# One store moved to the end of each step of the load queue, in an adaptive feed-forward kernel of two layers

## The reference, cut to what matters

```
x = x + L0_ffn( L0_cond(x, cond_128, ...), L0_ffn_weight )
    # L0_cond: grouped convolution along the columns, 9 taps, 4 groups, plus a context term and a bias
    # L0_ffn:  both sides rounded to int8 with a scale per row, product over 1024 columns, scaled back to f16
x = x + L1_ffn( L1_cond(x, cond_128, ...), W, b, A, Bmat, LiMEs )
    # L1_cond: a small MLP gives each batch mixing weights of 8 banks; a 64x64 matrix mixes the channels ("tokens") of each batch
    # L1_ffn:  H = tokens @ W.T + b, and z = tokens @ A; a gate over 8 experts scales z; result H + (z * mix) @ Bmat
```

## Time and profile before

| what | value |
|---|---|
| median of 3 runs | 613.61 us (612.49 to 615.41) |
| profiled execution, its own time | 613.3 us |
| its span in the profile | 611.5 us |
| TensorE (PE) busy | 604.1 us, 99% of the span |
| VectorE (DVE) busy | 433.3 us, 71% |
| ScalarE (ACT) busy | 357.0 us, 58% |
| GpSimd (POOL) busy | 375.0 us, 61% |
| DMA | 136.24 MB, mean 223 GB/s |

### The profile page before, as it was taken

One profiled execution on the slowest core, in us unless ns is written; L12 is line 12 of the kernel. 1 busy time (PEld: TensorE's weight loads), 2 busy tenths in 40 slices (PEclk: granted clock), 3 DMA queues, 4 the chain that ended last, 5 costly groups with the idle time before them and its releaser, 6 DMA issues.

```text
span 611.5 us, 16208 instructions
## 1 busy us (share of the span) xinstructions
PE 604.1 (99%) x6500; PEld 343.7 (56%) x6500; DVE 433.3 (71%) x883; ACT 357.0 (58%) x622; POOL 375.0 (61%) x252
## 2 busy tenths in 40 slices
PE   8999999999999999999999999999999999999998
PEld 5756667667776777765554444444444444444444
DVE  5988999978899999986877757754635454355543
ACT  3799998989999999876535234453233333321100
POOL 3436545546777666554888945989777659656200
PEclk9999999999999999999999999999999999999999
DMA  8989987878889999684183125765445445542111
GB/s 338 357 268 311 366 317 277 295 261 307 318 315 333 323 336 312 232 293 140 66 305 116 34 71 201 284 234 192 159 172 185 153 169 216 207 147 94 70 69 70
DMA packets 38632, 136.24 MB, mean 223 GB/s; under 512 B 5036, under 2 KB 5580, under 8 KB 38513
## 3 DMA queue, kind: packets, MB, share of 16 engines
q1 hardware_dynamic: 33518, 118.43, 54.6%
q10 hardware_dynamic: 5040, 16.78, 6.8%
HBM read 87.95 MB, written 47.24 MB: 221 GB/s over the span
## 4 chain that ended last, share of the span: by engine, by line
PE 87%; DVE 1%; issue 1%; ACT 0%; DVEq 0%
PE ps L908 42%; PE ps L612 16%; PE ps L517 9%; PE ps L709 7%; PE ps L596 4%; PE ps L890 2%; PE ps L581 2%; PE ps L657 2%; PE ps L652 1%; PE ps L621 1%; PE ps L625 0%; PE ps L692 0%; DVE yb L1459 0%; PE ps L677 0%; ACT zT L1096 0%
## 5 line engine op out<-in xcount | busy, mean ns | idle before, releaser
L612 PE MATMUL ps<-wqT,yq_both 128*128 128x512 bf16 x512 | 122.4, 379 | 0.3 <-DVE yb L1459 0.3
L1284 POOL TENSOR_TENSOR x<-x_in,f_all 128x512 f32<-128x512 f32 x64 | 74.3, 1162 | 51.1 <-DVE f_all L1496 51.0
L1288 POOL TENSOR_TENSOR x_split<-x_ph,x_split 128x1032 f16<-128x1032 f32 x25 | 53.7, 2148 | 55.5 <-ACT x_split L994 55.5
L1021 ACT ACTIVATE yv<-yb,yinv 128x128 f32<-128x128 f32 x256 | 77.8, 388 | 0.0
L1323 POOL TENSOR_TENSOR ring<-ring 128x512 f32<-128x512 f32 x56 | 72.8, 1300 | 4.3
L612 PEld LDWEIGHTS ps<-wqT,yq_both 128*128 128x128 bf16 x512 | 45.5, 99 | 46.3 <-issue 1.4
L517 PE MATMUL ps<-x_split,conv_h 128*64 128x256 f16 (+1 forms) x1248 | 60.0, 275 | 0.0
L1496 DVE SCALAR_TENSOR_TENSOR f_all<-ps,tok_scale,wsc_b 128x512 f16<-128x512 f32 x64 | 47.9, 749 | 16.7 <-PE ps L612 15.6
L517 PEld LDWEIGHTS ps<-x_split,conv_h 128*64 128x64 f16 (+1 forms) x1248 | 47.5, 108 | 9.7 <-issue 7.9
L1817 DVE SCALAR_TENSOR_TENSOR x_in<-ps,unscale,x_in 128x512 f32<-128x512 f32 x30 | 22.5, 750 | 39.9 <-PE ps L908 39.9
L1817 DVE SCALAR_TENSOR_TENSOR wst<-ps,unscale,wst 128x512 f32<-128x512 f32 x27 | 20.2, 750 | 36.7 <-PE ps L908 36.7
(11 more groups left out here) (351 smaller groups left out, 1321.5 us busy)
## 6 DMA issues: line engine op xcount, KB each, us to landing
x_in<-in_x SPq DMA_DIRECT2D x32, 512.0 KB, 6.0
x_scratch<-x SPq DMA_DIRECT2D x32, 512.0 KB, 3.7
x_ph<-in_x_phases SPq DMA_DIRECT2D x31, 516.0 KB, 5.2
x_scratch<-ring SPq DMA_DIRECT2D x26, 512.0 KB, 5.0
ring<-x_scratch SPq DMA_DIRECT2D x26, 512.0 KB, 5.2
x_in<-x_scratch SPq DMA_DIRECT2D x12, 512.0 KB, 3.5
out<-x_in ACTq DMA_DIRECT2D x12, 512.0 KB, 3.5
wst<-in_w_rows SPq DMA_DIRECT2D x10, 512.0 KB, 6.7
```

Of the source, the lines that this page charges most:

```text
L612: last = mm(acc_bank(t, h), yqT[:, t % 2, p, :], wqT[:, p, h * HALF:(h + 1) * HALF], start=p == 0, stop=p == PH - 1)
L1021: last = A(yv[:, s, :], yb[:, t % 2, s, :], ACT.Copy, scale=yinv[:, s:s + 1], bias=MAGIC)
L1284: g.tensor_tensor(x1[:, t % 2, s], x_in[:, t % 3, s], f16[:, s], ALU.add).then_inc(sem("x1_ready"), 1)
L1288: g.tensor_tensor(x_split[:, (t - SPLIT) % 2, 1, :], phases(t), x_split[:, (t - SPLIT) % 2, 0, :], ALU.subtract).then_inc(sem("xl_ready"), 1)
```

## The change

In each step the store of the mixed tokens, `save_x2(c - 4)`, is issued after `load_x`, `load_w` and `load_ws` instead of ahead of them. It still stands ahead of `load_t` and of all later transfers. No DMA is added or left out, and no wait is added or left out.

```diff
@@ -420,8 +420,6 @@
                     load_phases(c + LEAD + 1)
                 if c >= 3:
                     save_x1(c - 3)
-                if c >= 4 and c - 4 < SAVED:
-                    save_x2(c - 4)
                 if c == 2:
                     load_phases(4)
                 if 3 <= c < NT:
@@ -432,6 +430,8 @@
                     load_w(NL + split_steps.index(c + 2))
                 if c + 1 in sum_steps:
                     load_ws(sum_steps.index(c + 1))
+                if c >= 4 and c - 4 < SAVED:
+                    save_x2(c - 4)
                 if c == T_SCALE - 2:
                     load_t(0)
                 if c == T_SCALE:
```

## The result

The median is 615.89 us over 17 runs (612.64 to 620.46), against 613.11 us over 17 runs of the kernel before on the same chip. The ratio is 1.0041, with a 95% interval of 1.0024 to 1.0059: slower, by some 2.5 us. The time lies inside the range that was given, but the forecast was "no change", with 0.10 for slower by over 0.5%.

A forecast was written before the change was run, and what follows sets the result against it. TensorE was taken as the bound, busy 604.1 of 611.5 us. Every term was 0 us, so 613.3 us stayed 613.3; with the runs' median 0.3 us higher, 613.5 us was predicted, range 611.5 to 616.5 us.

The forecast's parts named there:

- What bounds the kernel: First stage, 50 to 250 us: TensorE busy 197.19 of 200 us, so reordering transfers finds 2.8 us at most.
- two or three gaps: Upper end of the range, 616.5 us, allowed for two or three 1.2 us TensorE gaps from late program fetches.
- SP waits nowhere new: SP's queue: the moved store's wait is always already over, so it holds up no loads; still no wait there.
- the loads of x and W: Loads issued 0.4 to 1.5 us earlier in each step; they were in time already, gain 0 us.
- the long issues: Issue on SP: long issues belong to the place in the burst, so they change lines; total unchanged, 0 us.
- the store's landing: Step 12: store at most 3.3 us later, its landing next asked for with over 37 us left; cost 0 us.
- The phases: Next load of phases, directly behind the moved store: taken as 0 us, upper bound 3.75 us in all.
- rival B: Phases land late behind the store's data in the early steps: up to 3.75 us slower, 617.1 us; chance 0.03.
- the sign that I had set: Prediction counts as wrong if TensorE's "issue" idle times grow by over 3 us.
- the fetches of TensorE's program: Late program code leaves TensorE idle, four gaps in the stage: taken as 0 us, bounds -2.0 to +9.6 us.
- rival A: Program fetches fall badly in heavy steps' mix and convolution: 1.2 us a gap, 617.1 to 622.9 us; chance 0.07.
- The bytes queued ahead are the same in both orders: Lower bound for the phase loads behind the moved store: same bytes ahead of them, so 0 us.

The follow-up runs named there:

- The two small-store kernels: Each mixed-token store and its load back cut to 64 of 1024 columns, in the kernels after and before: 611.51 us (0.9978) and 611.69 us (0.9980).
- runs 3 and 5: Mixed-token store behind the load of x but ahead of the loads of W: 615.29 us, 1.0048; store ahead of the x1 store: 623.51 us, 1.0170.
- the shift: Semaphore instructions added to TensorE's program: 32 give 1.0056 in the kernel after, 1.0004 in before; 128 give 1.0191 in after, 1.0045 in before.
- run 6: Mixed-token stores and their loads back cut to 64 of 1024 columns: store late 611.51 us, ratio 0.9978; store early 611.69 us, 0.9980.
- run 4: Store moved late only in the 14 steps with loads of W: 1.0032; late only in the other 12: 0.9990, against the kernel before.
- run 8: Row-sum copies of W one step earlier: kernel before 0.9995, kernel after 1.0073; kernel before with the load of x issued last: 1.0003.

## Why the prediction was wrong

**What bounds the kernel** held: TensorE, with 2.8 us to find in this stage. The two small-store kernels gain 1.3 us at most. The measured 615.89 us lie inside the range because the range had been widened for two or three gaps, not because the forecast of no change was right.

**The parts costed at nothing** mostly held, one by one. SP waits nowhere new, the loads of x and W have no one waiting, the long issues changed lines (the store's median issue is 0.775 us for 0.436, the load of x fell to 0.433 from 0.782), and the store's landing is asked for long after. The phases landed later (5.6 for 4.8 us), but ACT did not wait for them in this trace, and 0.8 us once in the second: rival B is not the loss. The "issue" times at block boundaries grew by 2.3 and 0.5 us in the two traces of the kernel after, so the sign that I had set, over 3 us, was too coarse for this loss.

**The step that failed** is the one on the fetches of TensorE's program, where I took 0 between -2.0 and +9.6 us. The mechanism was named, in rival A, but given 0.07. It measured about +2.5 us; in the traces the waits at block boundaries of the stage grew from 2.0 to 4.3 us. (The prices of rival A are not on one base: 617.1 us is 3.6 us above 613.5, and 622.9 us is 9.6 us above 613.3.) Two arguments misled me. First, the fetches take 1.0 us each whatever the queue does. That is true, and it is how long the packet is in transfer. What changes is when it starts: 1.27 us before TensorE runs dry in step 13 of the kernel before, 0.42 us before it in the kernel after. Second, I read the four gaps as a matter of luck, spread over 26 steps. Counting instructions would have shown that they sit at block boundaries in the mix, so each of these is open to a longer wait.

The page cited there, the Trainium skill, Runtime: NRT & Kernel Launch, section Instruction fetch mechanics, has blocks of 256 instructions, and the gaps at 193 and 194 modulo 256 agree. Its "mostly hidden" is right for most of the 52 fetches, but four of them showed a wait before and six after, and the loss lies in these. The Trainium skill, DMA: Bandwidth & Descriptors, section Queues, rings and completion order, has the engines take turns between queues packet by packet. I took from it that the order within SP's queue can't matter to a fetch. No trace here shows that turn-taking, and runs 3 and 5 say that the order does matter, at equal bytes; the measurement decides.

**"The bytes queued ahead are the same in both orders"** was true, and was no argument for equal delay: the store behind the loads takes 2.3 us longer to land (7.3 for 5.0 by the median), and the transfers that open the next step are slower.

Shown: the loss is TensorE waiting for program blocks (places modulo 256 in all traces, moved by the shift, and the stretch as long as the waits make it); the blocks are late because their packets start late; it needs the data of the store (run 6), in the heavy steps (run 4), and it is not had by moving a load (run 8). A part of it comes by way of the clock (12 of 63 runs against 3 of 196). Not shown: why the order of the store holds back the start of a fetch packet; the traces have the packets, not the request for them, and being behind a load, being apart from the x1 store and being in flight at the moment of the fetch are not told apart. Nor is it settled why the convolution weights land up to 1.8 us late at the start of some runs, the kernel before with the load of x last among them, with the same instructions up to there. In the trace of after 1.3 us came from that, so the sum over one trace need not equal the difference of the medians.

## What to carry to other kernels

When a tensor-bound kernel has short "issue" gaps inside a group of equal small matmuls, count TensorE's instructions up to them. If they repeat modulo 256, the program supply is on the critical path there, and the order of the large transfers around it can cost time though no engine waits for their data. Then look at when the fetch packet starts, not at how long it takes. A rule for the order does not follow from this one kernel. What it shows is that, in the heavy steps, the two stores issued one right after the other, ahead of the loads, was the best order, and that both moving one of them behind a load and sending it out 2.9 us ahead of the other cost time. Try such a move with repeated runs before you call it free.

## What the runs showed of the hardware

- The place of one 512 KB store in a step, at the same bytes and without any data wait, moved the time from 0.999 to 1.017 of the kernel before.
- The fetch packets of TensorE's program took 0.88 to 1.18 us at the 51 waits of over 0.4 us, and TensorE resumed 1.2 to 1.6 us behind their end. What varied was their start.
- A store issued behind loads of 512 KB lands later (7.3 us for 5.0 us), and so does the next step's first store (4.4 for 3.7 us).
- A semaphore instruction on TensorE cost 50 ns where eight waits, four instructions, stood behind each matmul of 512 columns (6.4 us for 128). Two instructions behind each cost 1.5 us for 128, and one behind each nothing visible.
- TensorE fell to its 1.2 GHz level after idle times of 1.75, 1.84 and 3.47 us in three traces, and stayed at 2.4 GHz after one of 2.02 us. Mean clock of the 10 us from 90 us on, in the kernel with the store ahead of the x1 store:

```profile
90.00:100.00 10.00, 7.98 (x93) 4.50 (x95) 4.26 (x14) 5.61 (x12) 4.24 (x3) 0.83 0.61 214
```
